# Order of instructions in the third context attention, and the place and queue of the swaps of the values' halves in four self attentions

## The chip, the cores and the metric

The kernel runs on one core of a Trainium2 chip. The metric is the device time of one execution in microseconds (us); the time before is the median of three runs. Engines are named as in the profile: PE (TensorE), DVE (VectorE), ACT (ScalarE), POOL (GpSimd) and SP, which here only issues DMAs.

## The reference

The program is four layers, each with an attention over a context of 1601 rows ("context attention"), an attention of the tokens over themselves, and a feed-forward part with experts. Two kinds of stages matter here. The third context attention is this one (x is 8 x 64 tokens of 256 features, z is 8 x 1601 context rows of 128 features, 16 heads of 16):

```python
Q = (x @ Wq.T).reshape(B, xN, NUM_HEADS, HEAD_DIM)
KV = (z @ Wkv.T).reshape(B, zN, 2, NUM_HEADS, HEAD_DIM)
attn = jnp.einsum('bqhd,bkhd->bhqk', Q, K) * SCALE
attn = jax.nn.softmax(attn, axis=-1)
O = jnp.einsum('bhqk,bkhd->bqhd', attn, V).reshape(B, xN, DIM)
return O @ Wo.T
```

The self attentions are softmax(q k^T) v over the 64 tokens of a batch, 16 heads; the first has a mask, the second and third rotary projections, the second and fourth biases.

## The kernel before

**Third context attention** (`paired_attention`). Its work is cut into 64 units of one batch and one pair of heads: 128 rows of queries (2 heads x 64 tokens) against 1601 keys. Two units are a couple, four couples a batch, so there are 32 couples. A first and a last part of the loop are written out, and the middle runs in a hardware loop. For a unit v the steps are:

- scores: four matmuls of 290, 512, 512 and 288 columns into the PSUM banks 0 to 3, which all units share. PE may overwrite the first half (802 columns) when the exponents of its first half have been read, and so with the second.
- maximum: DVE reduces each half and makes the negative maximum (`ntop`).
- exponents: ACT makes the probabilities of each half (tile `normed` for the even unit of a couple, `rooms` for the odd one).
- turn, keep, low: in four parts g = 0 to 3 (4, 4, 4 and 1 chunks of 128 keys) PE transposes the probabilities into a PSUM bank, ACT keeps a rounded copy (`pTh`), and DVE keeps the rest (`pTl`). A bank is free again when `low` is through.
- values: once for a couple, in the same four parts, each chunk in three passes (lines 616 to 618), with 256 columns for both units. `store` on DVE takes the result.

Beside it the keys of the batch after the next step are prepared. In each couple PE projects two key tiles (`key_tile`, 3 matmuls of 400 columns each), ACT drains each into the buffer `key_rows` (`keep_key`, line 1410; the profile calls it `weights`), and POOL splits it into high and low parts. Then SP copies the parts into the stacked keys with 12 DMAs (`move_half`, line 2569). Couples 0 and 2 of a batch fill half 0 of the key buffers, and couples 1 and 3 half 1. SP issues the moves of couples 0 and 1 one after the other, from the moment the scores of the batch's fourth unit are through (`sp.wait_ge(scores_ready, 8 * b + 4 + 2 * at)`), and those of couples 2 and 3 from the moment that its eighth is through, since they overwrite stacked keys that these units read. Half 0 of the key buffers may be overwritten when the move that reads it has landed; the drain of the first tile of a couple waits for that:

```python
act.wait_ge(key_ready, 8 * b + 2 * at + j + 1)
if j == 0 and at >= 2:
    act.wait_ge(moved[at % 2], MOVES * (2 * b + 1))
if j == 0 and at < 2 and not (first_step and i == 0):
    act.wait_ge(moved[at % 2], MOVES * 2 * b)
```

Both tiles of a couple go through PSUM bank 7, which the transposes use too, and PE waits for their drains (`key_kept`). The order of each engine is written out by hand in one `body` per engine.

**Self attentions** (`self_attention`, four of them). The values v are needed with the two halves of the partitions swapped as well. At the start of the block SP issues two DMAs for it (lines 535 and 536), and PE's first `values` waits for both. The stage ahead, `dense` or `rotary_projections`, makes q, k and v; v comes last in `dense`, and in the rotary form tile by tile between q and k.

Of the kernel before, what the change touches and what calls it, by code (L numbers as in the profile page):

```python
# [24 lines left out]
P = 128  # L25
# [10 lines left out]
HP = 32  # L36
# [73 lines left out]
def perceiver_kernel(nc, dram, packs, out):  # L110
    with ExitStack() as stack:
# [86 lines left out]
        def dense(products, pool=None, dve=None, act=None, sync=None, act_end=None, dve_end=None):  # L198
# [9 lines left out]
            with signals(nc, "product_ready", "taken_by_scalar", "taken_by_vector") as \  # L208
# [230 lines left out]
        def self_attention(qT, kT, v, oT, scale, dh, maskT=None, columns=None):  # L439
# [3 lines left out]
            names = ("chain", "swapped", "scores_ready", "shifted", "turned_ready", "exp_ready", "masked", "out_ready",  # L443
                     "normal_ready", "out_turned", "out_kept")
            with ExitStack() as own, signals(nc, *names) as \
                    (chain, swapped, scores_ready, shifted, turned_ready, exp_ready, masked, out_ready,
# [10 lines left out]
                with nc.Block() as block:  # L457
# [668 lines left out]
        def paired_attention(q, scale, keys, sums):  # L1126
# [8 lines left out]
            with ExitStack() as own, signals(nc, *names) as \  # L1135
# [15 lines left out]
                turned_bank = (4, 5, 7, 4), (5, 7, 4, 5)  # L1151
# [19 lines left out]
                with nc.Block() as block:  # L1171
# [98 lines left out]
                    def _(pe):  # L1270
                        def scores(u, step, first):
# [7 lines left out]
                            if u % 2 == 0:  # L1279
                                pe.wait_ge(staged, step * COUPLES + u // 2 + 1)  # L1280
                            k, at = (u // 2) % 2, (u % 2) * P
                            for n in range(4):
                                if n in (0, 2) and not (first and u == 0):
                                    pe.wait_ge(probs_ready if n else probs_half, v)
                                last = pe.matmul(flat[:, score_cols[n]], qs[:, k, at:at + P],
                                                 keys.stacked[:, u % PER, score_cols[n]], start=True, stop=True)
                                if n == 1:
                                    last.then_inc(scores_half, 1)
                            last.then_inc(scores_ready, 1)

                        def key_tile(u, step, j, final):

                            i, at = u // PER, (u // 2) % 4
                            for chunk, tile, n in key_tiles(i, at, final):
                                if n == j:
                                    if at == 0 and j == 0:
# [2036 lines left out]
```

## Time and profile before

| what | us |
|---|---|
| median of three runs (2257.9 to 2266.71) | 2265.95 |
| the profiled execution | 2265.01 |
| its span | 2263.2 |
| third context attention in it, about | 1697 to 2075 |
| self attentions, first values matmul | 63.57, 668.71, 1550.29, 2126.93 |
| granted TensorE clock, mean over the span | 0.945 |

PE is busy for 89% of the span, DVE for 62% and ACT for 50%. A busy time is the union of an engine's instructions; matmuls overlap, so what a matmul costs is the distance from its start to the next one's. An idle time in brackets stands ahead of an instruction, with the instruction that ended it. "SPq" rows are DMAs as SP issues them. In the tables by stretch, PEclk is the granted clock: 1.00 is 2.4 GHz and 0.50 is 1.2 GHz.

### The profile page before, as it was taken

The page shows a single profiled execution, that of the slowest core. Times are in us where ns is not written, and L with a number is a line of the kernel's source. Part 1 is how long each engine was busy: PE and PEld are TensorE (multiplying, and loading weights), DVE is VectorE, ACT ScalarE, POOL GpSimd, SP SyncE. Part 2 cuts the span into 40 slices and gives each one's busy share as a digit, 9 for nine tenths or more (in the row PEclk, how much of TensorE's full clock was granted, in tenths as well). Part 3 has the DMA queues.
Part 4 walks back from the last instruction along what each step waited for, and adds up shares of the span by engine and source line. Part 5 has one row for each costly group of instructions (what it writes and reads, how often), then busy time and mean ns, then how long its engine had stood idle before and what let it go on. Part 6 is the DMA issues. An engine that isn't in the chain of part 4 may idle for free. (4 is left out here: it accounts for less than half of the span.)

```text
span 2263.2 us, 42827 instructions
## 1 busy us (share of the span) xinstructions
PE 2018.8 (89%) x14978; PEld 1739.0 (77%) x14978; DVE 1392.2 (62%) x2718; ACT 1141.2 (50%) x2324; POOL 595.6 (26%) x536
## 2 busy tenths in 40 slices
PE   5877999999887998589899999988888998998898
PEld 2766999999566885278699999966767888887677
DVE  8455777777355443831577777745456777776466
ACT  3235666666423432321566666633446676665254
POOL 2323212221012330200322222102325555440034
PEclk9798999999996998689999999999998999999899
DMA  5252101000041213431110110002226555551022
GB/s 217 58 233 103 42 31 46 30 30 0 36 149 58 79 54 138 191 133 64 59 46 31 36 39 30 0 0 84 80 71 164 152 138 139 139 132 42 19 79 76
DMA packets 49603, 183.66 MB, mean 81 GB/s; under 512 B 9392, under 2 KB 14896, under 8 KB 46128
## 3 DMA queue, kind: packets, MB, share of 16 engines
q1 hardware_dynamic: 49456, 181.75, 25.0%
q8 instruction: 86, 1.41, 0.3%
q14 instruction: 61, 0.50, 0.1%
HBM read 125.72 MB, written 13.90 MB: 62 GB/s over the span
## 5 line engine op out<-in xcount | busy, mean ns | idle before, releaser
L616 PE MATMUL ps<-pTh,ch 128*128 128x256 f32 (+1 forms) x1248 | 382.3, 306 | 26.2 <-DVE pTl L1491 25.0
L1026 ACT ACTIVATE pTh<-ps 128x512 fp32r<-128x512 f32 (+1 forms) x512 | 235.8, 519 | 258.0 <-PE ps L926 257.7
L617 PE MATMUL ps<-pTl,ch 128*128 128x256 f32 (+1 forms) x1248 | 350.2, 281 | 0.0
L618 PE MATMUL ps<-pTh,cl 128*128 128x256 f32 (+1 forms) x1248 | 349.9, 280 | 0.0
L1084 DVE TENSOR_TENSOR pTl<-ps,pTh 128x512 fp32r<-128x512 f32 (+1 forms) x512 | 277.3, 583 | 83.8 <-ACT pTh L1026 83.2
L616 PEld LDWEIGHTS ps<-pTh,ch 128*128 128x128 f32 (+1 forms) x1248 | 236.1, 189 | 43.0 <-DVE pTl L1491 32.4
L617 PEld LDWEIGHTS ps<-pTl,ch 128*128 128x128 f32 (+1 forms) x1248 | 236.9, 190 | 0.0
L618 PEld LDWEIGHTS ps<-pTh,cl 128*128 128x128 f32 (+1 forms) x1248 | 235.9, 189 | 0.0
L616 PE MATMUL ps<-cTh,qh 128*128 128x512 f32 (+2 forms) x512 | 184.8, 361 | 16.7 <-POOL ql L880 11.9
L618 PE MATMUL ps<-cTh,ql 128*128 128x512 f32 (+2 forms) x512 | 179.9, 351 | 0.0
L617 PE MATMUL ps<-cTl,qh 128*128 128x512 f32 (+2 forms) x512 | 179.5, 351 | 0.0
L1071 DVE TENSOR_REDUCE top<-ps 128x1 f32<-128x802 f32 x128 | 126.3, 987 | 75.2 <-PE ps L618 75.2
L1491 DVE TENSOR_TENSOR pTl<-ps,pTh 128x512 fp32r<-128x512 f32 (+1 forms) x256 | 138.8, 582 | 47.8 <-ACT pTh L1431 47.1
L1431 ACT ACTIVATE pTh<-ps 128x512 fp32r<-128x512 f32 (+1 forms) x256 | 117.7, 514 | 56.1 <-PE ps L1312 56.0
L1073 DVE TENSOR_REDUCE top<-ps 128x1 f32<-128x799 f32 x128 | 125.9, 983 | 10.4 <-PE ps L618 3.8
L1015 ACT ACTIVATE normed<-ps,ntop 128x802 f32<-128x802 f32 (+1 forms) x128 | 117.8, 926 | 20.4 <-DVE ntop L1076 19.1
L926 PE MATMUL ps<-ident,probs 128*128 128x128 f32 (+1 forms) x832 | 122.0, 273 | 2.8 <-ACT probs L1015 1.7
L926 PE MATMUL ps<-ident,normed 128*128 128x128 f32 (+1 forms) x832 | 123.5, 275 | 0.4 <-DVE pTl L1084 0.4
L616 PEld LDWEIGHTS ps<-cTh,qh 128*128 128x128 f32 x512 | 97.9, 191 | 30.6 <-POOL ql L880 13.6
L616 PE MATMUL ps<-xh,wgh 128*128 128x512 f32 (+1 forms) x280 | 113.3, 405 | 5.4 <-DVE gated L1942 4.3
L1015 ACT ACTIVATE probs<-ps,ntop 128x802 f32<-128x802 f32 (+1 forms) x128 | 117.9, 937 | 0.0
L617 PE MATMUL ps<-xl,wgh 128*128 128x512 f32 (+1 forms) x280 | 112.6, 402 | 0.0
(406 smaller groups left out, 4613.2 us busy)
## 6 DMA issues: line engine op xcount, KB each, us to landing
stacked<-weights SPq DMA_DIRECT2D x168, 100.2 KB, 2.2
stacked<-weights SPq DMA_DIRECT2D x168, 100.0 KB, 2.2
w<-l1f_w_in SPq DMA_DIRECT2D x16, 1024.0 KB, 8.2
wg<-l0f_guide_in SPq DMA_DIRECT2D x10, 704.0 KB, 5.2
z<-ctx_in SPq DMA_DIRECT2D x8, 832.0 KB, 12.8
z<-z SPq DMA_DIRECT2D x8, 832.0 KB, 10.0
keys<-ctx_in SPq DMA_DIRECT2D x8, 832.0 KB, 10.7
zT<-zT SPq DMA_DIRECT2D x8, 801.0 KB, 9.1
```

The lines of the kernel that those rows point to most:

```text
L616: pe.matmul(out, high, moving_high, start=start, stop=False)
L617: pe.matmul(out, high, moving_low, start=False, stop=False)
L618: return pe.matmul(out, low, moving_high, start=False, stop=stop)
L926: last = pe.transpose(ps[0:w, turned_bank[slot][g], k * P:(k + 1) * P], probs[slot][:, chunk * P:chunk * P + w], ident[:])
L1015: nc.scalar.activation(probs[slot][:, cols], flat[:, cols], ACT.Exp, bias=ntop[:, slot:slot + 1], scale=scale, accum_out=sums[:, bass.ds(2 ...
L1026: nc.scalar.activation(pTh[0:w, PARTS[g][0]:PARTS[g][0] + n, slot, :], ps[0:w, turned_bank[slot][g], 0:n * P].rearrange("p (k r) -> p k r" ...
L1071: dve.tensor_reduce(top[:, slot, 0:1], flat[:, half_cols[0]], AX.X, ALU.max).then_inc(top_step, 1)
L1073: dve.tensor_reduce(top[:, slot, 1:2], flat[:, half_cols[1]], AX.X, ALU.max)\
L1084: dve.tensor_tensor(pTl[0:w, at, slot, :], ps[0:w, turned_bank[slot][g], 0:n * P].rearrange("p (k r) -> p k r", r=P), pTh[0:w, at, slot, : ...
L1431: nc.scalar.activation(pTh[0:w, PARTS[g][0]:PARTS[g][0] + n, slot, :], ps[0:w, turned_bank[slot][g], 0:n * P].rearrange("p (k r) -> p k r" ...
L1491: dve.tensor_tensor(pTl[0:w, at, slot, :], ps[0:w, turned_bank[slot][g], 0:n * P].rearrange("p (k r) -> p k r", r=P), pTh[0:w, at, slot, : ...
```

## The change

In the third context attention the same instructions come in another order, and PSUM banks are used differently:

- The banks of the four turned parts go from (4, 5, 7, 4) and (5, 7, 4, 5) to (7, 4, 5, 4) and (7, 4, 7, 5), and the two key tiles have a bank each (4 and 5) instead of sharing 7.
- Each unit's scores are issued as two halves. For the even unit the first half comes ahead of everything, then one turned part and both key tiles, then the second half.
- Both key tiles stand at the couple's start, on PE and on ACT. Before, the first stood after `values(1)` and the second behind the next transposes.
- On ACT and DVE a part of the turned tiles' work stands between the two halves of exponents and of maxima.

The waits of the key drains on `moved` and SP's program are as before.

In the self attentions SP's two swaps are gone. ACT issues them in the stage ahead, once the last tile of v is drained (and the column of ones written). In `dense` v now comes first and is drained by ACT alone; in the last self attention DVE drained two of its four tiles before.

```diff
-                turned_bank = (4, 5, 7, 4), (5, 7, 4, 5)
+                turned_bank = (7, 4, 5, 4), (7, 4, 7, 5)
+                turn_place, low_place = ((2, 1, 3, 4), (1, 2, 4, 3)), ((2, 1, 4, 3), (1, 2, 4, 3))
+                key_bank = 4, 5
...
-                                pe.wait_ge(probs_half, v)
-                                turn_second(0, v - 1)
-                                scores(u, step, first)
+                                first_scores(u, step, first)
+                                pe.wait_ge(low_kept, 4 * v - 6)
+                                turn(0, v - 1, 1)
...
+                                key_tile(u, step, 0, final)
+                                pe.wait_ge(low_kept, 4 * v - 4)
+                                key_tile(u, step, 1, final)
+                                second_scores(u, step, first)
+                                key_bank_free(u, step, 0, final)
+                                turn(1, v - 1, 1)
+                                key_bank_free(u, step, 1, final)
+                                turn(3, v - 1, 1)
+                                pe.wait_ge(low_kept, 4 * v - 3)
+                                turn(2, v - 1, 1)
                                 values(0, c - 1, i, first and u == 2, new_batch)
-                                turn_second(3, v - 1)
                                 values(1, c - 1, i)
-                                if key_tiles(u // PER, (u // 2) % 4, final):
-                                    pe.wait_ge(low_kept, 4 * v - 2)
-                                key_tile(u, step, 0, final)
-                                scores(u + 1, step, first)
-                                turn_first(0, v)
-                                turn_first(1, v)
-                                key_tile(u, step, 1, final)
+                                first_scores(u + 1, step, first)
+                                second_scores(u + 1, step, first)
+                                turn(1, v, 0)
+                                pe.wait_ge(low_kept, 4 * v)
+                                turn(0, v, 0)
+                                turn(2, v, 0)
                                 values(2, c - 1, i)
-                                key_bank_free(u, step, final)
-                                turn_first(2, v)
                                 values(3, c - 1, i)
-                                turn_first(3, v)
+                                pe.wait_ge(low_kept, 4 * v + 1)
+                                turn(3, v, 0)
...
+        def swap_halves(engine, v, swapped):
+
+            engine.dma_start(v[0:S, :, 1], v[S:P, :, 0]).then_inc(swapped, 16)
+            engine.dma_start(v[S:P, :, 1], v[0:S, :, 0]).then_inc(swapped, 16)
...
-                    @block.sync
-                    def _(sp):
-                        sp.dma_start(v[0:S, :, 1], v[S:P, :, 0]).then_inc(swapped, 16)
-                        sp.dma_start(v[S:P, :, 1], v[0:S, :, 0]).then_inc(swapped, 16)
...
+                            if n == NT - 1 and taken_first is not None:
+                                scalar.wait_ge(taken_by_scalar, NT)
+                                taken_first(nc.scalar)
...
+                            if t == NT - 1:
+                                act.wait_ge(values_kept, NT)
+                                act.wait_ge(counted, NT)
+                                swap_halves(nc.scalar, v, swapped)
```

**ACT in the third context attention**, from the exponents of a couple's even unit (`normed`) on. `pTh` is a kept part, `weights_1` the drain of a key tile. Before:

```order
L1420 ACTIVATE normed,rooms<-ps,ntop 128x802
L1420 ACTIVATE normed,rooms<-ps,ntop 128x799
L1431 ACTIVATE pTh<-ps 65x128
L1410 ACTIVATE weights_1<-ps 128x400
L1431 ACTIVATE pTh<-ps 128x4x128 x2
L1410 ACTIVATE weights_1<-ps 128x400
L1420 ACTIVATE rooms<-ps,ntop 128x802
L1420 ACTIVATE rooms<-ps,ntop 128x799
L1431 ACTIVATE pTh<-ps 128x4x128
L1431 ACTIVATE pTh<-ps 65x128
```

And now, from the exponents of the odd unit (`rooms`) to those of the next even one:

```order
L1429 ACTIVATE rooms<-ps,ntop 128x802
L1440 ACTIVATE pTh<-ps 128x4x128
L1440 ACTIVATE pTh<-ps 65x128
L1429 ACTIVATE rooms<-ps,ntop 128x799
L1440 ACTIVATE pTh<-ps 128x4x128
L1419 ACTIVATE weights_1<-ps 128x402
L1419 ACTIVATE weights_1<-ps 128x400
L1440 ACTIVATE pTh<-ps 128x4x128
L1440 ACTIVATE pTh<-ps 65x128
L1429 ACTIVATE normed,rooms<-ps,ntop 128x802
```

Both drains now stand ahead of the even unit's exponents and of three of the odd unit's four kept parts, where the first drain stood behind all of these.

**PE in the same stage now**, at the start of a couple; `stacked,qs` are scores, `ident,rooms` turned parts of the odd unit before, `wkh` and `wkl` key tiles:

```order
L1298 MATMUL ps<-stacked,qs 128x290
L1298 MATMUL ps<-stacked,qs 128x512
L1321 MATMUL ps<-ident,rooms 128x128 x4
L619 MATMUL ps<-cTh,wkh 128x402
L620 MATMUL ps<-cTl,wkh 128x402
L621 MATMUL ps<-cTh,wkl 128x402
L619 MATMUL ps<-cTh,wkh 128x400
L620 MATMUL ps<-cTl,wkh 128x400
L621 MATMUL ps<-cTh,wkl 128x400
L1298 MATMUL ps<-stacked,qs 128x512
L1298 MATMUL ps<-stacked,qs 128x288
L1321 MATMUL ps<-ident,rooms 128x128 x4
```

The key tiles moved from the couple's middle to its start, and the turned part behind the second half of the scores needs the first key tile's bank.

## Rows read from the trace of the kernel before

**Rows 1.** Busy times by stretch: PE, weight loads, DVE, ACT, POOL, PEclk, DMA, GB/s.

```profile
1800.00:1850.00 50.00, 45.94 (x345) 43.01 (x344) 37.31 (x65) 35.02 (x79) 26.23 (x31) 1.00 0.57 144
```

**Rows 2.** Waits from 1700 to 2065: us in total, times, longest us.

```profile
PE ps L616 <- DVE pTl L1491: 27.0, 30, 2.8
```

**Rows 3.** Timeline of PE over one couple: start, us, instruction, count, idle before.

```profile
1821.94 0.39 PE L616 MATMUL ps<-pTh,ch 128*128 128x256 f32 x1 [0.81 <-DVE pTl L1491]
...
1828.90 0.98 PE L1285 MATMUL ps<-stacked,qs 96*128 96x290 f32 x4
1830.09 1.09 PE L1312 MATMUL ps<-ident,rooms 128*128 128x128 f32 x8 [0.20 <-DVE pTl L1491]
...
1832.44 0.27 PE L1312 MATMUL ps<-ident,rooms 128*65 128x128 f32 x1
1833.52 0.39 PE L616 MATMUL ps<-pTh,ch 128*128 128x256 f32 x1 [0.81 <-DVE pTl L1491]
...
1835.04 0.35 PE L616 MATMUL ps<-cTh,wkh 128*128 128x400 f32 x1
...
1835.60 0.90 PE L1285 MATMUL ps<-stacked,qs 96*128 96x290 f32 x4
1836.34 1.04 PE L1312 MATMUL ps<-ident,normed 128*128 128x128 f32 x8
```

**Rows 4.** SP's twelve DMAs of two moves, and the time to landing.

```profile
1836.53 8.07 SPq L2569 DMA_DIRECT2D stacked<-weights  x12
...
1954.79 7.52 SPq L2569 DMA_DIRECT2D stacked<-weights  x12
...
DMA to landing us min/median/max: 2.2/2.2/2.9
```

**Rows 5.** ACT's drain of the first key tile of the next couple.

```profile
1847.45 0.51 ACT L1410 ACTIVATE weights<-ps 128x402 f32<-128x402 f32 x1 [0.80 <-PE ps L618]
```

**Rows 6.** Idle times of PE, and the stretches around them as in rows 1.

```profile
1890.96 0.58 PE L616 MATMUL ps<-pTh,ch 128*128 128x256 f32 x1 [1.97 <-DVE pTl L1491]
...
594.46 0.79 PE L318 MATMUL ps<-weights,oT 128*128 128x256 f32 x1 [3.54 <-PEq L1557]
...
1589.11 0.77 PE L616 MATMUL ps<-xh,wgh 128*128 128x512 f32 x1 [4.28 <-DVE gated L1942]
...
1891.00:1894.20 3.20, 3.20 (x15) 3.20 (x16) 3.11 (x5) 0.98 (x2) 1.29 (x3) 0.50 0.68 163
1894.30:1898.00 3.70, 3.70 (x29) 3.61 (x28) 1.69 (x3) 2.15 (x7) 0.83 (x2) 1.00 0.65 156
594.50:600.50 6.00, 6.00 (x14) 4.83 (x15) 1.04 (x3) 1.38 (x2) 0.00 (x0) 0.50 0.00 1
...
1589.20:1593.80 4.60, 4.60 (x11) 3.63 (x12) 2.37 (x4) 2.11 (x4) 2.37 (x1) 0.50 0.38 114
```

**Rows 7.** Timeline of the self attentions and of the stages ahead of them.

```profile
661.40 0.62 SPq L535 DMA_DIRECT2D v<-v  x1
...
665.95 1.09 ACT L559 ACTIVATE probs<-ps 128x512 f32<-128x512 f32 x2 [3.77 <-PE ps L480]
...
668.71 1.83 PE L507 MATMUL ps<-v,probs 64*64 64x17 f32 x64 [2.36 <-DMA v<-v]
...
674.86 1.91 PE L507 MATMUL ps<-v,probs 64*64 64x17 f32 x64 [0.78 <-ACT oT L567]
...
1550.29 1.12 PE L507 MATMUL ps<-v,probs 64*64 64x17 f32 x64 [0.83 <-ACT probs L559]
...
1554.29 1.12 PE L507 MATMUL ps<-v,probs 64*64 64x17 f32 x64 [0.80 <-ACT oT L571]
...
1542.65 0.60 ACT L2180 ACTIVATE qT<-ps 128x512 f32<-128x512 f32 x1 [1.06 <-PE ps L2113]
...
2116.53 0.69 ACT L395 ACTIVATE kT<-ps,weights 128x512 f32<-128x512 f32 x1 [2.75 <-PE ps L231]
...
2119.98 0.38 ACT L435 ACTIVATE v<-ps 128x256 f32<-128x256 f32 x1 [1.34 <-PE ps L231]
```

More of the change, by code:

```diff
@@ L1270, in _, with first_scores @@
                     def _(pe):
-                        def scores(u, step, first):
+                        def first_scores(u, step, first):
                             i = u // PER
@@ L1280, in scores, with second_scores @@
                                 pe.wait_ge(staged, step * COUPLES + u // 2 + 1)
+                            if not (first and u == 0):
+                                pe.wait_ge(probs_half, v)
+                            score_half(u, 0).then_inc(scores_half, 1)
+                        def second_scores(u, step, first):
+                            if not (first and u == 0):
+                                pe.wait_ge(probs_ready, step * UNITS + u)
+                            score_half(u, 1).then_inc(scores_ready, 1)
@@ L1281, in scores, with score_half @@
+                        def score_half(u, half):
                             k, at = (u // 2) % 2, (u % 2) * P
-                            for n in range(4):
-                                if n in (0, 2) and not (first and u == 0):
-                                    pe.wait_ge(probs_ready if n else probs_half, v)
+                            for n in (2 * half, 2 * half + 1):
                                 last = pe.matmul(flat[:, score_cols[n]], qs[:, k, at:at + P],
                                                  keys.stacked[:, u % PER, score_cols[n]], start=True, stop=True)
-                                if n == 1:
-                                    last.then_inc(scores_half, 1)
@@ L1289, in scores @@
-                            last.then_inc(scores_ready, 1)
+                            return last
                         def key_tile(u, step, j, final):
                             i, at = u // PER, (u // 2) % 4
-                            for chunk, tile, n in key_tiles(i, at, final):
-                                if n == j:
-                                    if at == 0 and j == 0:
-                                        pe.wait_ge(low_ready, 2 * (2 * step + i) + 1)
-                                    if j == 1:
-                                        pe.wait_ge(key_kept, 8 * (2 * step + i) + 2 * at + 1)
-                                    project_keys(pe, keys, chunk, tile, 7).then_inc(key_ready, 1)
@@ L1302, in key_bank_free @@
-                        def key_bank_free(u, step, final):
+                            tiles = key_tiles(i, at, final)
+                            if tiles:
+                                if at == 0 and j == 0:
+                                    pe.wait_ge(low_ready, 2 * (2 * step + i) + 1)
+                                project_keys(pe, keys, tiles[j][0], tiles[j][1], key_bank[j]).then_inc(key_ready, 1)
+                        def key_bank_free(u, step, j, final):
                             i, at = u // PER, (u // 2) % 4
@@ L1356, in body @@
                                 if first and u == 0:
[L1357 to L1360 removed]
+                                    for n in range(2):
+                                        first_scores(u + n, step, first)
+                                        second_scores(u + n, step, first)
@@ L1409, in keep_key @@
                             cols = K_COLS[tile]
-                            nc.scalar.activation(key_rows[:, cols], ps[:, 7, 0:cols.stop - cols.start], ACT.Copy)\
+                            nc.scalar.activation(key_rows[:, cols], ps[:, key_bank[j], 0:cols.stop - cols.start], ACT.Copy)\
                                 .then_inc(key_kept, 1)
```

143 lines of the change are left out of this document (72 added, 71 removed).

## The prediction, made blind

> **What bounds the kernel now.** I read the page's busy times first (they stand in the section on the profile): PE is busy for 89% of the span, so a gain has to come out of PE's waits, or a loss has to make new ones. The tables by stretch show where the third context attention stands [rows 1]: PE 45.94 of 50 us, DVE 37.31, ACT 35.02, at full clock. So PE is nearly the bound there, and the other engines have room. Its waits [rows 2] are 27.0 us in 30 pieces of `values` for DVE's low parts, about one in each of the 32 couples. The timeline of one couple [rows 3] shows what a couple costs: from 1821.94 to 1833.52, 11.58 us.
>
> Of these PE works how long? Distances from start to start give the pieces: four score matmuls 0.74 (1835.60 to 1836.34), so a half 0.37; a key tile 0.56 (1835.04 to 1835.60); four chunks of values 1.52 right after a wait (1833.52 to 1835.04), 1.43 otherwise, and the last chunk 0.36; a turned part of four 0.43 with the hand-over to the next group, the single one 0.12. A couple is then 4 x 0.37 + 2 x 0.56 + 3 x 1.43 + 0.36 + 6 x 0.43 + 2 x 0.12 = 10.07 us. The rest is two waits [rows 3]: after the single turned part at 1832.44 (0.12 of work) until 1833.52, that is 0.96; and after the scores at 1828.90 (0.74 of work) until 1830.09, 0.45; and 0.09 to start again. Sum 11.57. **So at most 1.5 us a couple, 47 us in 31 couples, can be won here.**
>
> **The new order without the copies.** I walked PE, ACT, DVE, POOL and SP through a couple in both orders with these pieces (ACT: a half of exponents 0.92, a kept part 0.49, a drain 0.42 to the next and 0.51 to its end; DVE: maxima 0.90 and 1.01, `ntop` 0.13, a low part 0.60). The old order comes out at 11.56, with both waits in their place. In the new one DVE's low part g = 1 is ready before `values(1)` needs it, since `first_maximum` and one low part run while PE still projects keys; what is left are waits of 0.02 to 0.15 for low parts. **A couple would take 10.3 us, 1.27 less.**
>
> **The copies of the keys.** Here the new order makes a wait that the old one just missed. The drain of the first key tile of couples 0 and 2 of a batch waits until the move that reads this half of `key_rows` has landed, and SP starts that move when the scores of the last unit of the couple before are through. The rows of the move [rows 4]: the first DMA goes out at 1836.53, right after those scores; the twelve take SP 8.07 us, so the last begins some 0.6 us before 1844.60, and it lands 2.2 us later, at 1846.2. That is 9.7 us. In the other move shown SP took 7.52, which gives 9.1. I reckon with 9.4. In the old order the drain comes at 1847.45 [rows 5], 10.9 us after the scores, behind the couple's scores, its exponents and half its values. The cover is 1.2 us, and that is why no row shows ACT waiting for a move.
>
> In the new order the drain comes much sooner after those scores: three turned parts 1.29, `values(2)` 1.43, `values(3)` 0.36, the single part 0.12, half a unit's scores 0.37, a turned part 0.43, a key tile 0.56, some 0.15 of waits and 0.1 to its end: 4.8 us. So ACT stands from 4.8 to 9.4, **4.6 us, once in two couples**. Queued behind the drain on ACT are the second drain, kept parts 1 and 3, the exponents of the even unit and kept part 2. PE still issues the second half of the scores, and then its next turned part waits for the drained bank (`key_bank_free`), so PE stands for about the same 4.6 us, and DVE with it. SP's own program cannot catch up: it starts from those same scores.
>
> Two couples then take 2 x 10.3 + 4.6 = 25.2 us, where they take 23.1 now: 2.1 more. The drains concerned are those of couples 2, 4, ... 26: 13. Sum 13 x 2.1 = 27 us lost. The five intervals left gain: the four couples of the last batch, without key tiles, about 0.6 each, another 1.3; together 4. **Stage: +23 us** at full clock. Bounds: with the move at 9.1 us +19, at 9.7 us +27.
>
> **The clock.** PE now stands for 4.6 us in 25. What follows such a gap [rows 6]: in this very stage a gap of 1.97 ended at 1890.96, and until 1894.20 the granted clock was 0.50 (1.2 GHz); PE did 15 matmuls in 3.20 us there and 29 in 3.70 at 1.00, so 0.60 of the pace. A gap of 3.54 ended at 594.46 with the clock at 0.50 until 600.5, one of 4.28 at 1589.11 until 1593.8. So 3.3, 6.0 and 4.7 us of low clock behind a gap, each costing 0.4 of itself: 1.3, 2.4 and 1.9 us. The path behind the drain is PE's own work (turned parts, values, scores up to the scores that start the next move), so it is paid in full. I take their mean, 1.9, **13 x 1.9 = 24 us**; ends 0 (the gaps leave the clock alone) and 13 x 2.4 = 31.
>
> The Trainium skill bears on this (TensorE: Matmul & The Clock Gate, HAM oscillation — how this bites in real kernels): it describes matmuls that wait for a DMA in each tile and start each tile cold, at half the rate. By that rule every one of the 13 gaps would be followed by low clock, as I assume; the trace has no repeated gap of this size, so it can't tell.
>
> **The swaps.** In the second self attention PE's first values stand at 668.71, having waited 2.36 us for `v<-v`, while the exponents were done at 665.95 + 1.09 = 667.04 [rows 7]. An early swap takes away 1.65 us. In the third (1550.29) the exponents came last, and in the first the masked copy on POOL and in the fourth the exponents: nothing there. Cost: ACT issues two DMAs; no row shows ACT issuing one. SP needs 0.62 for one [rows 7], so some 1.3 us and a wait for its own drain; it has idle stretches of 1.06 (1542.65) to 2.75 us (2116.53) in these stages to hide it, so 0 to 0.3 us a stage. In the last self attention the end of `dense` is now a drain of k at 0.69 instead of v at 0.38: +0.3. Net -1. Beyond that the second self attention ran from that gap on at low clock: a tile took 6.15 us (668.71 to 674.86), where the third, at full clock, took 4.00 (1550.29 to 1554.29). Keeping the clock up would give 2.15 x 3 tiles, about 6.5; the fourth self attention lost the clock without any swap in the way, so I count half, 3. **Swaps: -4 us**, between -9 and +2.
>
> The Trainium skill also says (DMA: Bandwidth & Descriptors, Issuing engines are not separate DMA queues) that issuing from another engine saves only sequencer time, since all DMAs share 16 engines. By it the queue is worth nothing and the earlier place everything, which is how I count; the sum stays.
>
> **Sum.** 2265.0 (profiled execution; the median of the runs is 2265.95, 1 us above) + 23 + 24 - 4 = **2308 us, 1.9% slower.**
>
> **Rivals.** (1) *The gaps leave the clock alone, or cost less than the swaps give.* 2265 + 23 + 0 - 4 = 2284, up to 2292 with one short low stretch after every other gap. For it: PE has worked at full rate for 20 us before each gap. Against: the 1.97 us gap was enough. Chance 0.2. (2) *The copies are through in time, and the order gives what it has.* 2265 - 31 x 1.27 - 4 = 2222, or with a small rest of the wait up to 2254. It would take a move that lands 4.8 us after its scores instead of 9.7: SP would have to issue its DMAs in half the time, or the drain would have to slip back by 4.6 us for another reason. The row of SP speaks flatly against it: 12 DMAs, 8.07 us. The point at which the change turns from gain to loss lies in between: a stall of 2 x 1.27 = 2.5 us in two couples, so a move of 7.3 us. Chance 0.07. (3) *Break-even:* the wait is partly hidden because PE's path is longer than my walk says (more waits on low parts), and the clock stays up: 2255 to 2277. Chance 0.05. (4) *The low clock lasts longer*, 8 us behind each gap, at 0.4 each 3.2 us: 2265 + 27 + 13 x 3.2 - 1 = 2333. Chance 0.12. The forecast itself, stall and clock both, has 0.56.
>
> **How the numbers follow.** Range 2280 to 2332: from the case without a clock loss and with the full gain of the swaps to the upper ends of both terms and a swap that costs instead of gains (2265 + 27 + 31 + 2 = 2325), with some room for rival 4; below it lie rivals 2 and 3, above it half of rival 4. A measurement here tells 0.5% (11 us) from no change. Slower by more than that: the forecast, rivals 1 and 4, 0.88. Same: 0.05. Faster: 0.07.
>
> **What the new profile would show.** If right: the distances of the scores alternate between some 10.3 and 15 to 17 us; ACT's drain of the first key tile in every second couple comes about 9.7 us after the scores and shows an idle time of 4 to 5 us; PE shows 13 gaps of 4 to 5 us ahead of turned parts in `rooms`, ended by that drain; PEclk in the stage falls from 1.00 to about 0.9; the stage takes 400 to 430 us instead of 377. In the other couples `values(1)` no longer waits for DVE. In the second self attention PE's wait for `v<-v` is gone. I am wrong if the drains show no idle time (step: the copies), if PEclk stays at 1.00 (step: the clock), or if couples without the stall still take over 11 us (step: the walk).

## The result, and the profile after

| | us |
| --- | --- |
| before, median of 4 runs | 2261.93 (2256.58 to 2266.71) |
| after, median of 4 runs | 2310.47 (2308.47 to 2314.58) |
| after / before | 1.0218, 95% interval 1.0185 to 1.025 |
| after, profiled execution | 2310.07, its span 2308.2 |
| forecast | 2308, range 2280 to 2332 |

The change makes the kernel 2.2% slower. Where the time went is read by marks that both traces have. For the third context attention I take two matmuls of PE: the second unit's scores at its start, and the first output projection behind it. Columns here and in the next blocks: start us, us, instruction, count, idle time before it and who ended it. In the profile before:

```profile
1702.97 1.61 PE L1285 MATMUL ps<-stacked,qs 96*128 96x290 f32 x3 [2.88 <-ACT normed L1420]
2089.05 1.19 PE L318 MATMUL ps<-weights,oT 128*128 128x256 f32 x2 [1.82 <-PEq L1557]
```

and in the profile after:

```profile
1704.18 1.61 PE L1298 MATMUL ps<-stacked,qs 96*128 96x290 f32 x3 [3.01 <-ACT normed L1429]
2140.20 1.10 PE L321 MATMUL ps<-weights,oT 128*128 128x256 f32 x4 [1.82 <-PEq L1568]
```

From mark to mark the stage took 386.1 us before and takes 436.0 us after: **+49.9 us**, while the span grew by 45.0. The rest is +1.2 ahead of the stage and -6 behind it. So the loss is in this one stage. Its largest waits in the table of waits after (us in total, times, longest; stretch 1700 to 2138):

```profile
PE ps L1321 <- ACT weights L1419: 53.9, 13, 4.6
ACT weights L1419 <- DMA stacked<-weights: 52.3, 12, 4.9
```

L1419 is the drain of a key tile (`keep_key`), L1321 a turned part. Neither row is there before, where PE's largest wait was that for the low parts [rows 2]. One stall in the timelines, first SP with its copies, then ACT's drain, then PE:

```profile
1747.69 15.69 SPq L2592 DMA_DIRECT2D stacked<-weights  x24
```

```profile
1757.40 0.90 ACT L1419 ACTIVATE weights<-ps 128x402 f32<-128x402 f32 x2 [4.76 <-DMA stacked<-weights]
```

```profile
1752.88 0.53 PE L1298 MATMUL ps<-stacked,qs 96*128 96x512 f32 x2
1757.96 2.18 PE L1321 MATMUL ps<-ident,rooms 128*128 128x128 f32 x9 [4.55 <-ACT weights L1419]
```

Two moves of twelve DMAs stand in a row on SP (15.69 us for 24, so 7.85 for one). The drain comes 9.7 us after the first of them, having waited 4.76 us, and PE stands for 4.55 us between the second half of a unit's scores and the next turned part. This stall is one of the longer ones: the mean is 4.4 us for the waits of ACT (52.3 us in 12) and 4.1 for those of PE (53.9 in 13). Before, this drain came 10.9 us after the scores and waited for no copy [rows 4, 5].

Behind each gap the clock is low. Tables by stretch, as in rows 1: the stretch of rows 1 in the profile after, then the one right behind the gap above, then the one up to the next gap.

```profile
1800.00:1850.00 50.00, 42.12 (x288) 39.74 (x286) 30.58 (x53) 28.82 (x64) 22.78 (x26) 0.86 0.52 129
1756.20:1762.90 6.70, 4.94 (x23) 4.94 (x24) 1.58 (x3) 3.96 (x9) 2.78 (x4) 0.50 0.68 160
1763.20:1783.20 20.00, 17.95 (x135) 16.65 (x133) 15.91 (x27) 12.53 (x27) 9.61 (x10) 1.00 0.39 105
```

PE was busy for 45.94 of these 50 us and is busy for 42.12. The clock is at 0.50 (1.2 GHz) from within the gap until 1762.9, 5.0 us behind its end, and at 1.00 again until the next gap. That happens 13 times.

In the second self attention the wait that the early swap was to remove is still there. ACT issues the swaps at 658.64, PE waits for them until 670.65:

```profile
658.64 0.64 ACTq L444 DMA_DIRECT2D v<-v  x1
659.31 0.63 ACTq L445 DMA_DIRECT2D v<-v  x1
...
670.65 1.90 PE L515 MATMUL ps<-v,probs 64*64 64x17 f32 x64 [2.45 <-DMA v<-v]
```

Before it was 2.36 us [rows 7].

From the second mark to the end the kernel takes 168.0 us after and took 174.1 before. This gain is one of the clock: after, it stays at 1.00 from 2064 to 2300; before, it was at 0.95 from 2090 to 2250. The first of these two stretches is the longer one, so only their clocks are compared.

```profile
2064.00:2300.00 236.00, 212.62 (x1800) 178.06 (x1798) 151.26 (x315) 115.79 (x234) 58.43 (x63) 1.00 0.21 59
```

```profile
2090.00:2250.00 160.00, 148.62 (x1246) 122.12 (x1245) 93.78 (x214) 66.28 (x130) 49.37 (x49) 0.95 0.20 58
```

### The profile page after: what moved, and what is told of

The parts are those of the page before. It is cut to its first block and busy times, and to the rows that moved or that the text cites. A ratio compares the mean times of both kernels' runs of the same rounds, so it can differ in the third digit from the quotient of the medians.

```text
span 2308.2 us, 42776 instructions
## 1 busy us (share of the span) xinstructions
PE 2036.9 (88%) x14978; PEld 1758.9 (76%) x14978; DVE 1392.0 (60%) x2716; ACT 1145.4 (50%) x2326; POOL 595.4 (26%) x536
## 5 line engine op out<-in xcount | busy, mean ns | idle before, releaser
L619 PE MATMUL ps<-pTh,ch 128*128 128x256 f32 (+1 forms) x1248 | 387.6, 311 | 1.2 <-DVE pTl L1087 1.2
L620 PE MATMUL ps<-pTl,ch 128*128 128x256 f32 (+1 forms) x1248 | 357.8, 287 | 0.0
L621 PE MATMUL ps<-pTh,cl 128*128 128x256 f32 (+1 forms) x1248 | 356.8, 286 | 0.0
L619 PEld LDWEIGHTS ps<-pTh,ch 128*128 128x128 f32 (+1 forms) x1248 | 245.7, 197 | 10.7 <-DVE pTl L1087 8.3
L620 PEld LDWEIGHTS ps<-pTl,ch 128*128 128x128 f32 (+1 forms) x1248 | 245.6, 197 | 0.0
L621 PEld LDWEIGHTS ps<-pTh,cl 128*128 128x128 f32 (+1 forms) x1248 | 244.2, 196 | 0.0
L1321 PE MATMUL ps<-ident,rooms 128*128 128x128 f32 (+1 forms) x416 | 70.9, 318 | 57.5 <-ACT weights L1419 53.9
## 6 DMA issues: line engine op xcount, KB each, us to landing
z<-z SPq DMA_DIRECT2D x8, 832.0 KB, 10.3
keys<-ctx_in SPq DMA_DIRECT2D x8, 832.0 KB, 10.9
```

Source lines behind the costliest of these rows:

```text
L619: pe.matmul(out, high, moving_high, start=start, stop=False)
L620: pe.matmul(out, high, moving_low, start=False, stop=False)
L621: return pe.matmul(out, low, moving_high, start=False, stop=stop)
L1321: last = pe.transpose(ps[0:w, turned_bank[slot][g], k * P:(k + 1) * P], probs[slot][:, chunk * P:chunk * P + w], ident[:])
```

## The experiments

The theory: the loss is all in the third context attention, 27 us less 4 from the drain that now comes ahead of the landing of SP's copies, and 24 us from the low clock behind each of the 13 gaps. The rivals: the early swaps carry a part of it; the stall alone is all of it and the clock costs little; something else in the new order makes the wait. "Stage" is the distance between the two marks above, in the profiled execution of each kernel. Each ratio is taken to runs of before made beside that kernel; the medians of these lie between 2260.7 and 2265.9 us.

| kernel | stage, us | median, us | ratio to before, 95% interval |
| --- | --- | --- | --- |
| before | 386.1 | | |
| after | 436.0 | 2310.5 | 1.0218 (1.0185 to 1.025) |
| e1 order only | 432.4 | 2306.8 | 1.0201 (1.0167 to 1.0235) |
| e2 swaps only | 389.2 | 2265.4 | 1.0025 (1.0007 to 1.0044) |
| e3 order only, PE kept busy | 408.4 | 2284.4 | 1.0109 (1.0077 to 1.0141) |
| e4 after, two sets of key rows | 359.7 | 2234.1 | 0.9893 (0.9862 to 0.9925) |
| e5 order only, two sets | 353.5 | 2231.6 | 0.9866 (0.9828 to 0.9904) |
| e6 old order, two sets | 386.5 | 2264.7 | 1.0005 (0.9989 to 1.0021) |
| e7 order only, 8 DMAs a move | 377.6 | 2254.9 | 0.996 (0.9943 to 0.9978) |
| e8 as e5, context load by ACT | 352.8 | 2227.2 | 0.9849 (0.9804 to 0.9894) |
| e9 as e2, contexts loaded later | 389.2 | 2272.3 | 1.0049 (1.003 to 1.0067) |
| e10 before, contexts loaded later | 385.8 | 2272.8 | 1.004 (1.0023 to 1.0057) |
| e11 as e8, contexts loaded later | 353.0 | 2238.9 | 0.9896 (0.9875 to 0.9916) |
| e12 as e8, contexts loaded among the experts | 351.7 | 2221.1 | 0.9825 (0.9802 to 0.9848) |

### The two parts apart: e1 and e2

e1 is the kernel before with the new order of `paired_attention`; e2 is the changed kernel with the old one.

> The kernel before with the new order of the third context attention alone; the swaps stay on SP's queue in their old place. Theory (the loss is the stall behind the copies of the keys and the low clock after it, both of them in this stage): the stage takes 50 us more, as in the changed kernel, with 13 PE gaps of 4 to 4.6 us; whole kernel 2305 to 2315 us, +2.0 to +2.3%. Rival (the early swaps carry part of the loss, by ACT's queue or by a shifted clock): under 2300 us.

> The changed kernel with the old order in the third context attention: the early swaps alone. My prediction gave the swaps -4 us (between -9 and +2). Theory after the trace of the changed kernel (the swap in the second self attention lands at the same moment as before, so PE still waits there for the values): within 2 us of the kernel before, 2260 to 2266 us. Rival (the swaps give what I predicted, and the late landing in the one trace was chance): 2255 to 2258 us, no wait of PE for v in the second self attention.

e1 measured 2306.8 us, with the stage 46.3 us longer and 13 gaps of PE. The order is the loss. e2 measured 0.25% more than before, and not less. Its swaps, issued at 659.54, were waited for until 671.70, as in the changed kernel:

```profile
671.70 1.91 PE L515 MATMUL ps<-v,probs 64*64 64x17 f32 x64 [2.59 <-DMA v<-v]
```

So the -4 us of the prediction are not there. In its profile e2's stage is 3.1 us longer though none of its lines is changed. The difference lies where the loop over the batches begins again, first e2, then the same place before:

```profile
1893.93 1.57 ACT L1434 ACTIVATE pTh<-ps 128x512 fp32r<-128x512 f32 x3 [4.44 <-issue]
```

```profile
1889.59 1.57 ACT L1431 ACTIVATE pTh<-ps 128x512 fp32r<-128x512 f32 x3 [2.31 <-PE ps L1312]
```

In e2 ACT waits 4.44 us for nothing that the profile shows, and PE 4.09 behind it, where it was 1.97 [rows 6]. e9 (early swaps) has 4.09 there too, e10 (old swaps) 1.71. The longer idle time comes with the early swaps in both pairs of the old order, and in the pair of the new order below as well (e4 and e5). The profile's table of DMAs has a hint: beside the data it lists transfers of the kind "instruction", two of them inside e2's 4.44 us (1889.5 to 1893.9) and one inside the 2.31 us of before (1887.3 to 1889.6). So ACT may have waited for its own instructions; no run tests that. The spans of the two profiles differ by only 0.7 us (2263.9 and 2263.2), since the part behind the second mark took 4 us less in e2, where less of it was at low clock. Of e2's 12 runs none is below 2259.7 us, of 17 runs of before six are; the last section on experiments comes back to these.

### Stall and clock apart: e3

Ahead of the wait for the drained bank PE turns the identity into columns that nobody reads:

```
+                                if (u // 2) % 2 == 0 and key_tiles(u // PER, (u // 2) % 4, final):
+                                    for _ in range(40):
+                                        pe.transpose(ps[:, 6, 2 * P:3 * P], ident[:], ident[:])
                                 key_bank_free(u, step, 0, final)
```

> The new order alone (as e1), and ahead of the wait for the drained bank, in the 13 couples where it stalls and in the other couples with even number that have key tiles, PE turns the identity 40 times into unused columns of a bank; nothing reads them. So ACT stalls as before but PE does not stand idle. Theory (half of the loss is low clock behind each gap): granted clock 1.00 through the stage, the stall stays about as long, ACT still waits some 4 us at 13 drains; 20 to 26 us less than e1, so 2286 to 2292 us. Rival (the clock costs little, the stall is all of it): within 8 us of e1, or above it by what the added transposes cost.

ACT still waits for the copies as long as in e1, but PE nearly not for ACT (waits 1700 to 2100):

```profile
ACT weights L1419 <- DMA stacked<-weights: 55.8, 13, 5.6
PE ps L1318 <- ACT weights L1419: 1.7, 3, 1.0
```

and the clock, over 300 us of the stage, in e3 and then in e1:

```profile
1740.00:2040.00 300.00, 299.07 (x2354) 284.95 (x2353) 205.67 (x355) 193.57 (x424) 147.24 (x167) 1.00 0.52 130
```

```profile
1740.00:2040.00 300.00, 253.10 (x1740) 237.35 (x1740) 191.76 (x331) 180.56 (x397) 135.36 (x155) 0.89 0.48 122
```

PE does 40 useless transposes a stall, and the kernel is 22.4 us faster than e1, the stage 24.0 us. What is left, +22.3 us in the stage, is about the stall at full clock. It is not exact: the transposes outlast the drain in 7 of 12 stalls, by 0.2 to 0.3 us, which adds some 2 us to it (an estimate from these times). Two couples take 25.34 us in e3 (eleven periods of the scores, 278.7 us) and 27.26 in e1 (299.9 us). The rival by which the clock costs little is out.

### The copies: e4 and its control e6

The change keeps one set of `key_rows` for both halves of a batch. e4 gives each half its own, with its own high parts and semaphores:

```
-                            if j == 0 and at >= 2:
-                                act.wait_ge(moved[at % 2], MOVES * (2 * b + 1))
-                            if j == 0 and at < 2 and not (first_step and i == 0):
-                                act.wait_ge(moved[at % 2], MOVES * 2 * b)
+                            if j == 0 and not (first_step and i == 0):
+                                act.wait_ge(moved[at], MOVES * b)
```

> The changed kernel with a second set of key rows and their high parts, one for each half of a batch, so that a drain waits only for the move of the batch before; order, engines and number of copies are the same. Theory (the drain's wait for the copies is the cause of all the loss, and without it the order gives what the walk of a couple says): no wait of ACT for a move, no gaps of PE over 2 us, clock 1.00, a couple 10.3 us, the stage 38 us shorter than before; whole kernel 2222 to 2232 us. Rival 1 (something else in the new order, such as the two key tiles in a row, makes the wait): still 2300 us or more. Rival 2 (the walk is too short, waits on low parts take back what the order gives): 2250 to 2265 us.

> Control: the kernel before, old order and old swaps, with the second set of key rows alone. Theory (in the old order the copies land 1.2 us before the drain asks for them, so a second set has nothing to save, and the gain of e4 belongs to the order): the same time as before within 3 us. Rival (the copies or the buffers cost the old order something that the waits do not show): 5 to 25 us faster than before.

ACT waits for no move any more, and e4 is 1.1% faster than before, 76 us faster than after. Its 2234.1 us lie just above the 2222 to 2232 that were expected. The clock is at 1.00, and PE is busy for 48.82 of 50 us in the stretch of rows 1:

```profile
1800.00:1850.00 50.00, 48.82 (x379) 46.14 (x378) 40.62 (x71) 38.28 (x84) 31.18 (x34) 1.00 0.59 154
```

The old order gets nothing from the second set (e6, 1.0005): there the copies were in time. So the wait of the drain for the copies, with the low clock behind it, and nothing else in the new order, made the loss, and without it the order is a gain. e4's stage is 26.4 us shorter than before and not 38 as expected. Couples that wait for nothing take 10.3 to 10.4 us, as walked, but PE waits 5.4 us in 4 for POOL's low part of the next batch's context, and there is a gap of 3.3 us at the head of the loop with low clock after it. Two couples' first scores in e5, 10.40 us apart:

```profile
1801.57 0.96 PE L1309 MATMUL ps<-stacked,qs 96*128 96x290 f32 x4
...
1811.97 0.95 PE L1309 MATMUL ps<-stacked,qs 96*128 96x290 f32 x4
```

### How much of a move is issue: e7

e7 is e1 with 8 DMAs in each move instead of 12; the second copy of the high parts is left out.

> The new order alone (as e1) with 8 DMAs in each move of keys instead of 12: the second copy of the high parts is left out, so the stacked keys hold rows of an earlier batch there. Theory (SP's time to issue sets the stall): a move is 2.7 us shorter, the 13 waits of ACT for a move fall from 4.3 us to about 1.6, PE gaps of 1.3 to 1.9 us; at full clock two couples take 22.6 us, 13 x 2.7 = 35 us less than e1, 2272 us; down to 2250 us if the low clock behind gaps of that size goes too. Rival (a move is set by what the DMA engines carry or by the landing of the last one, not by issue): the waits shrink by under 1 us each, 2290 us or more.

The waits of ACT for a move fell from 4.3 to 1.8 us each (e1, then e7):

```profile
ACT weights L1416 <- DMA stacked<-weights: 56.0, 13, 5.4
```

```profile
ACT weights L1416 <- DMA stacked<-weights: 22.0, 12, 2.7
```

Four DMAs less take 2.5 us off each wait, 0.62 us for one, which is what SP needs to issue one [rows 7]. Issue sets the stall. Two couples take 22.9 us, just under the 23.1 of the old order, and the kernel is 0.4% faster than before. The point of break-even lies near the 2.5 us of the prediction and somewhat below it: where the clock stayed up, two couples with a gap of 1.4 us took 22.4 us, so a gap of about 2.1 would make 23.1. With gaps of 1.4 to 2.5 us the clock mostly stayed up:

```profile
1740.00:2020.00 280.00, 258.94 (x1927) 241.52 (x1927) 212.83 (x368) 200.31 (x441) 143.23 (x167) 0.99 0.41 107
```

That is why the time is nearer to the lower end of what was expected (2250) than to 2272. The profiled execution is the fastest of e7's ten (2244.5 us, the median is 2254.9), so for the others the clock in this stage is not known.

### What is late next: e5 and e8

e5 is e4 with the swaps where they were.

> As e4 (new order, a second set of key rows for the other half of a batch) with the swaps on SP's queue in their old place. Theory (the early swaps give nothing anywhere; e2 measured them at +0.25%, between 0.07 and 0.44%): 2228 to 2234 us, 0 to 6 us less than e4. Rival (e2's difference was a chance of its loop boundary in the third context attention): equal to e4, 2234 us.

It measured 2231.6 us; the intervals of the two overlap. In the profiles its stage is 6.3 us shorter than e4's, some 3 us of it at the head of the loop again (a gap of 1.2 us against 3.3, and low clock behind the longer one; ACT idles there once, for 2.2 us, and twice in e4, for 2.1 and 1.8). In both the context's load is late, here in e4: it goes out on SP behind a move, POOL waits for it, PE for POOL.

```profile
1734.33 0.58 SPq L1198 DMA_DIRECT2D weights<-ctxT_in  x1
```

```profile
1739.42 1.53 POOL L1231 CAST cTh<-weights 128x1602 fp32r<-128x1602 f32 x1 [2.23 <-DMA weights<-ctxT_in]
```

```profile
1744.30 0.42 PE L631 MATMUL ps<-cTh,wkh 128*128 128x402 f32 x1 [1.71 <-POOL cTl L1234]
```

e8 issues this load from ACT, in the third couple of a batch:

```
+                                if at == 2 and not final:
+                                    b = 2 * step + i
+                                    act.wait_ge(low_ready, 2 * b + 2)
+                                    nc.scalar.dma_start(raw[:, 0:KEVEN], dram["ctxT"][bass.ds(b + 2, 1)]
+                                                        .rearrange("b p k -> (b p) k")).then_inc(raw_landed, 16)
```

> As e5, and the load of the next batch's transposed context is issued by ACT's queue in the third couple of a batch, where its buffer is free, instead of by SP behind the second move of keys. In e4 the load goes out 10 us later than the buffer is free; POOL waits for it 8.8 us in 6 waits, and PE for POOL's low part 5.4 us in 4. Theory (with the stall gone SP's queue is the next bound, by the place of this load): those waits go, 4 to 8 us less than e5. Rival (ACT's issue of 0.64 us and its wait in the middle of a couple cost what the load gives): within 2 us of e5.

PE's wait for POOL's low part is gone, the median 4.4 us lower, but the intervals overlap, and in the profiles the stage is only 0.7 us shorter: at the head of the loop e8 has a gap of 1.9 us, with low clock behind it, where e5 has one of 1.2 us and no low clock. e8's four runs lie at 2220.7, 2222.2, 2232.3 and 2233.1 us; the profiled one is of the lower pair and gained 8.6 us on e5 in another stage, the second self attention and its experts, by chance as the next section shows. Whether this edit gains anything by itself stays open.

### Why an early swap is late: e9 to e12

Ahead of the second self attention SP issues the loads of two contexts for the one-head cross attention, 6.5 MB. e9 (with early swaps) and e10 (with the old ones) issue them behind it.

> As e2 (early swaps, old order) and the loads of the first two contexts for the one-head cross attention (6.5 MB) go to SP's queue behind the second self attention instead of ahead of it. Theory (the swaps of the second self attention land late because these loads are in front of them in the DMA engines, whoever issues the swaps): the swap lands within 4 us of its issue at 659, PE does not wait for v, and without that gap the clock stays at 1.00 through the stage; 6 to 9 us less than e2, 2256 to 2259 us. Rival 1 (the landing is set by something else): the wait stays, time as e2. Rival 2 (the wait goes, the clock falls anyway): 1.5 to 2 us less than e2.

> The kernel before with the same later loads, swaps on SP's queue in their old place. Theory (the loads are the whole delay; an early issue adds nothing once they are gone): a swap issued at 661.4 lands by 665, ahead of the exponents' end at 667.0, so no wait either; the same time as e9 or up to 5 us less, 2252 to 2257 us. Rival (the swap needs both, the early issue and the free engines): PE still waits 1 to 2 us for v, within 2 us of before.

Median us from issue to landing of the swaps, in the profile after and in e9:

```profile
v<-v ACTq DMA_DIRECT2D x2, 272.0 KB, 10.6
```

```profile
v<-v ACTq DMA_DIRECT2D x2, 272.0 KB, 3.6
```

So it was the loads. In e10 the swaps issued by SP at 661.54 were in time too, though in its profile the exponents came 1.6 us later than in before, since the clock was low during the scores; at full clock the swaps in the old place were just in time in e11 and e12 below. No kernel without these loads in front has the wait. PE's values then come right behind the exponents, and the clock stays at 1.00 through the stage (e9; before, it was at 0.50 from 668.9 to 692.7, behind the wait):

```profile
667.60 1.12 PE L515 MATMUL ps<-v,probs 64*64 64x17 f32 x64 [0.83 <-ACT probs L562]
```

```profile
602.00:689.00 87.00, 72.81 (x828) 53.39 (x826) 41.07 (x94) 29.93 (x61) 16.24 (x16) 1.00 0.13 43
```

Yet both kernels are slower than before, at 2272.3 and 2272.8 us, and the 2256 to 2259 and 2252 to 2257 that were expected were wrong. The loads now stood in front of the experts' weights, and ACT and PE waited there (e9):

```profile
728.06 1.38 ACT L1845 ACTIVATE wgh<-wg 128x1408 fp32r<-128x1408 f32 x1 [15.72 <-DMA wg<-l0f_guide_in]
```

```profile
732.26 0.74 PE L619 MATMUL ps<-xh,wgh 128*96 128x512 f32 x1 [14.93 <-DVE gated L1945]
```

e11 has the same edit on e8, and e12 puts the first of the two loads behind those of the third expert and the second behind the last expert's.

> e8 (new order, second set of key rows, context load by ACT's queue, old swaps) with the same later loads. Theory: the two changes lie in different stages and add, 5 to 8 us less than e8: 2218 to 2222 us, 1.8 to 2.0% less than before. Rival (the later loads are missed by the one-head cross attention, which starts later): 2227 us or more.

> As e11, but the two loads of contexts stand neither ahead of the second self attention nor ahead of its experts' loads: the first goes out among the experts' loads after those of the third expert, the second behind the last of them. In e9 and e11 they delayed the experts' loads instead (ACT waited 15.7 us for one, PE stood 14.9 us). Theory (the swaps' wait and the low clock after it are worth 8 to 9 us, as e9 showed up to 690, and only the place of the loads took it back): no wait of PE for v, no gap of 15 us at 717; 6 to 9 us less than e8's share of before, so 1.9 to 2.1% less than before. Rival (the experts or the one-head cross attention miss the loads there too): no better than e8, 1.5% or less.

e11 came out worse than e8 for the same reason (2238.9 us, expected were 2218 to 2222). e12 has neither wait: the values at 669.76 follow the exponents, and the clock is up.

```profile
669.76 1.12 PE L519 MATMUL ps<-v,probs 64*64 64x17 f32 x64 [0.83 <-ACT probs L571]
```

```profile
604.00:690.00 86.00, 72.97 (x829) 53.55 (x827) 40.11 (x93) 29.95 (x61) 15.15 (x15) 1.00 0.14 44
```

Between two waits of `norms` that both profiles have, ahead of the second self attention and behind its experts, e12 takes 203.4 us and before 212.4, so 9.0 us are gained there. First e12, then before:

```profile
643.59 0.44 PE L299 MATMUL ps<-ident,normed 128*128 128x128 f32 x2 [1.84 <-DVE normed L372]
...
846.97 0.44 PE L299 MATMUL ps<-ident,normed 128*128 128x128 f32 x2 [1.80 <-DVE normed L278]
```

```profile
641.00 0.44 PE L287 MATMUL ps<-ident,normed 128*128 128x128 f32 x2 [1.84 <-DVE normed L360]
...
853.36 0.69 PE L287 MATMUL ps<-ident,normed 128*128 128x128 f32 x2 [1.61 <-DVE normed L266]
```

**e12 is the fastest kernel of this study: 2221.1 us, 0.9825 of before (0.9802 to 0.9848).** It is 1.75% faster, less than the 1.9 to 2.1% that were expected. The distance of its median to e8's is 6 us and their intervals overlap, so that e12 is faster than e8 is not shown. One reason is that e8 has the same gain by chance in some executions: between the same two waits its profile takes 203.7 us, where e12's takes 203.4 and e5's 212.3. In it, as in e6's, the clock was low during the scores, so the exponents came 2 us later, the swap had landed, and the clock then stayed up. In e6 (661.30 to 667.80 are the scores):

```profile
661.30:667.80 6.50, 6.32 (x146) 5.91 (x146) 2.45 (x2) 1.28 (x1) 2.00 (x1) 0.50 1.00 289
668.00:691.00 23.00, 16.94 (x456) 14.43 (x455) 14.48 (x27) 8.39 (x19) 5.45 (x3) 1.00 0.02 4
```

e8's runs in two pairs, 10 us apart, and e12's within 8 us (2216.7 to 2224.5) fit that. It would also explain why the runs of before spread over 18 us (2249 to 2267 in the first series). I have no profile of such a run of before, so it stays an argument, and it does not say why e2's do not reach as low.

## Why the prediction was right, and where not

**The copies.** Right in mechanism and size. The drain was walked to come at 4.8 us with the move landing at 9.4, a wait of 4.6, 13 times. The profile has 9.7 and 4.76 for one, 4.4 in the mean, and 13 PE gaps of 3.9 to 4.6 us. e3 puts the whole term at about full clock at +22.3 us where the sum had +23. That term has two parts. The 13 periods of two couples with a stall lie between the same two first scores in every kernel, first before, then after:

```profile
1725.51 0.61 PE L1285 MATMUL ps<-stacked,qs 96*128 96x290 f32 x2
...
2027.85 0.62 PE L1285 MATMUL ps<-stacked,qs 96*128 96x290 f32 x2
```

```profile
1723.15 0.60 PE L1298 MATMUL ps<-stacked,qs 96*128 96x290 f32 x2
...
2079.02 0.61 PE L1298 MATMUL ps<-stacked,qs 96*128 96x290 f32 x2
```

That is 302.3 us before and 355.9 after, and 330.1 in e3: 2.1 us a period at full clock, as predicted, and 4.1 with the clock, where 2.1 and 1.9 were. The other part, -4 us, was put down mostly to the last batch. There is no gain there: from these last scores to the second mark it is 61.2 us in both kernels. The start of the stage, up to these first scores, takes 3.6 us less after (5.1 in e3) instead, so this -4 was met by luck.

e4, e6 and e7 show the cause from three sides: take the dependence away and the loss turns into a gain, the old order has no use for it, and fewer DMAs shorten the wait by their time of issue.

**The clock.** Right. 24 us were predicted, 13 times 1.9; e1 less e3 is 24.0 us in the stage and 22.4 in the medians, 1.9 a period (27.26 less 25.34 us). That it agrees so closely is in part luck: in e1 four of the 13 low stretches were only half as long as the others, and for the changed kernel, where all were long, the distance to e3 is 27.6 us (436.0 less 408.4). The mean of three gaps elsewhere [rows 6] was a good guide, and the repeated cold start that the Trainium skill describes (TensorE: Matmul & The Clock Gate, HAM oscillation — how this bites in real kernels) is what the trace shows, with 0.50 behind every one of the 13 gaps. Rival 1 (the gaps leave the clock alone) is out at this size of gap. It was partly right for e7: there gaps of 1.4 to 2.5 us mostly left the clock up, although one of 1.97 did not in the profile before.

**The walk of a couple.** 10.3 us predicted, 10.3 to 10.4 measured in e4 and e5 where nothing is waited for, and as much in the changed kernel's couples without a stall, which alternate with couples of 16.8 to 17.4 us (15 to 17 were predicted). But rival 2's sum, 31 times 1.27 without the stall (39 us), promised more than the 33 us of e5 and e8: the distance of the two orders is 0.1 us a couple smaller than in the walk (11.52 measured before over twelve couples, 10.36 in e8 over thirteen), the last batch gave nothing up to the second mark, and with PE faster the load of the next context became late, which no step had looked at.

**The swaps.** This step failed: "an early swap takes away 1.65 us", and with it -4 us. It assumed that the time from issue to landing is the DMA's own, so that an earlier issue lands earlier. The landing was set by the 6.5 MB issued before it: counted from the start of the stretch ahead (641.00 before, 642.87 after) ACT issued the swap 4.6 us sooner, at 658.64 instead of 661.40, and it was waited for until 670.65 instead of 668.71, which is no sooner by the same count. I had named what the Trainium skill says on it (DMA: Bandwidth & Descriptors, Issuing engines are not separate DMA queues: all share the same engines) and drawn from it only that the queue is worth nothing, not that the earlier place is worth nothing either. The other half of the step, that a wait gone keeps the clock up, held: 9.0 us in e12, where 8.15 had been worked out (1.65 + 6.5) and 4 taken. What the swaps did cost, +0.25% by e2 (0.07 to 0.44%), lies by the profiles outside of what I had priced, at the head of the loop in another stage; its cause is open.

**The sum** came close, 2308 for 2310.5, on a base that turned out 4 us lower (2261.9): the change added 48.5 us where 43 were predicted. The 5.5 us between are about the -4 of the swaps and where the clock happened to be low (the stage took 436.0 in the changed kernel and 432.4 in e1, and the part behind it gained 6). The lower base hid the missing 4 us of the swaps, so that the forecast came within 2.5 us of the measured time is luck; that it came within 5.5 us in the change is not.

## What to carry to other kernels

When an order is changed, look for waits that are met today with a small cover (here 1.2 us of 10.9) and follow them on every queue; a buffer that is read by a chain of small DMAs is busy for the time of their issue, and a second buffer can turn the same order from 2% slower into 1.3% faster. Price a gap of PE twice, by itself and by the clock behind it: here the two were equal. Look at what was issued ahead of a small DMA: here it was as late as the large loads before it, from whichever of the two engines it was issued. Moving it earlier gained nothing, and where the loads were moved, they delayed what stood behind their new place until they were spread.

## What the runs showed of the hardware

- At 13 gaps of 3.9 to 4.6 us the granted clock was 0.50 for 6.8 us each time in the changed kernel, some 5 us of it after the gap; in e1 (gaps of 3.9 to 5.3 us) four of the thirteen had only 3.4 us. Gaps of 1.4 to 2.5 us (e7, one execution) were followed by low clock in two cases of 13.
- 40 transposes of the identity in each stall, 0.11 us each, were enough to keep the clock at 1.00 from 1740 to 2040, although they compute nothing (e3).
- A chain of 12 small DMAs keeps its source buffer busy for the time of their issue: 7.85 us for 12, and 0.62 us less waiting for each one left out (e7).
- A DMA of 272 KB took 10.6 us from issue to landing with 6.5 MB ahead of it and 3.6 us without (after, e9).
- A change in other stages lengthened the start of a loop: ACT's idle time there was 4.44 us in e2, with two transfers of the kind "instruction" in it, and 2.31 us in the same place before, with one. What ACT waited for is not shown.
